# A two-layer graph convolution: unrolled chunks without index copies, dense nodes in pairs of 1024, layer 2 written in node layout

## The reference, cut to what matters

```
x: (100000, 96)   src, dst: (25000,), sorted by dst   edge_attr: (25000, 32)

def conv(x, W_msg, W_edge, W_root, b):
    msg = x[src] @ W_msg + edge_attr @ W_edge
    agg = segment_max(msg, dst, 100000)       # 0 where a node has no edge
    return agg + x @ W_root + b
c1 = leaky_relu(conv(x, W1...));  c2 = leaky_relu(conv(c1, W2...))   # slope 0.01
out = layernorm(x + c2)           # over the 96 features, no scale or bias
```

## Time and profile before

| | us |
|---|---|
| median of 3 runs | 1723.31 |
| fastest, slowest run | 1714.04, 1755.0 |
| profiled execution: span, first to last instruction | 1697.5 |
| around the span, to the median | 25.8 |
| PE busy (in it weight loads, PEld, overlapping) | 978.8 (438.7) |
| DVE busy | 1044.2 |
| ACT busy | 666.9 |
| POOL busy | 1055.8 |
| granted clock of PE, mean | 0.746 |

### The profile page before, as it was taken

How to read it: one execution, slowest core, us unless ns; L and a number is a source line. 1 busy time by engine, 2 the same in 40 slices (tenths; PEclk the granted TensorE clock), 3 DMA queues, 4 the chain that set the end, 5 groups by cost and what they waited for, 6 DMA issues and landing times.

```text
span 1697.5 us, 21367 instructions
## 1 busy us (share of the span) xinstructions
PE 978.8 (58%) x3038; PEld 438.7 (26%) x3038; DVE 1044.2 (62%) x3881; ACT 666.9 (39%) x1717; POOL 1055.8 (62%) x1182
## 2 busy tenths in 40 slices
PE   3476866666666465687778778454343443334441
PEld 1233433233333232332322223222111111111210
DVE  2356666555555465679999999665544555445553
ACT  1345654444444354568888888400000000000000
POOL 5566656455545545617877767666667766677665
PEclk9678877778777777889999999755655655556555
DMA  6366756556555455755444444533333333233320
GB/s 172 93 183 207 240 178 181 174 175 194 175 177 184 146 179 171 220 177 185 157 153 154 152 146 154 164 111 106 104 95 94 107 99 104 79 102 99 107 74 21
DMA packets 142053, 245.87 MB, mean 145 GB/s; under 512 B 31470, under 2 KB 70120, under 8 KB 142022
## 3 DMA queue, kind: packets, MB, share of 16 engines
q1 hardware_dynamic: 103462, 161.26, 30.4%
q0 software_dynamic: 31360, 45.90, 11.5%
q10 hardware_dynamic: 7200, 38.40, 6.0%
HBM read 122.70 MB, written 125.07 MB: 146 GB/s over the span
## 4 chain that ended last, share of the span: by engine, by line
issue 34%; DVE 15%; PE 15%; another core or an unknown queue 15%; ACT 11%; POOL 4%; DMA 1%; DVEq 1%; ACTq 1%; POOLq 1%
ACT ob L686 5%; PE ps L529 5%; PE ps_r L529 4%; DVE stat L820 3%; PE ps_t L519 2%; POOL out L302 2%; PE ps_m L529 2%; DVE c1t L780 2%; DVE mv L831 2%; ACT c2t L647 2%; POOL g_src L295 2%; DVE c2t L780 2%; DVE stage L923 1%; DVE mx L790 1%
## 5 line engine op out<-in xcount | busy, mean ns | idle before, releaser
L686 ACT ACTIVATE ob<-ps_y,shift,rstd 128x96 f32<-128x96 f32 x784 | 273.7, 432 | 139.9 <-DVE shift L859 71.4
L820 DVE BATCH_NORM_STATS2 stat<-ps_y 128x6 f32<-128x96 f32 x784 | 147.0, 248 | 192.4 <-remote 141.1
L302 POOL DMA_INDIRECT agg_table<-stage,now_end x196 | 221.2, 1128 | 68.5 <-issue 68.2
L302 POOL DMA_INDIRECT out<-stage,now_end x196 | 200.4, 1022 | 60.0 <-issue 59.1
L295 POOL DMA_INDIRECT g_src<-in_x,now_gat x196 | 195.8, 999 | 63.0 <-issue 62.9
L295 POOL DMA_INDIRECT g_dst<-in_x,now_gat x196 | 195.2, 996 | 59.7 <-issue 59.1
L529 PE MATMUL ps<-xtb,wr 97*96 97x512 f32 x392 | 224.1, 655 | 11.0 <-ACT c1t L647 2.9
L295 POOL DMA_INDIRECT g_src<-agg_table,now_gat x196 | 196.8, 1004 | 52.9 <-issue 52.6
L529 PE MATMUL ps<-c1t,wr 97*96 97x512 f32 x392 | 212.4, 625 | 11.5 <-issue 10.3
L519 PE MATMUL ps_t<-ident,g_src 128*96 128x128 f32 x392 | 90.2, 374 | 209.9 <-DMA g_src<-agg_table,now_gat 176.7
L655 ACT ACTIVATE std<-mv,epsc 128x4 f32<-128x4 f32 x245 | 74.6, 305 | 296.5 <-issue 185.5
(11 more groups left out here) (54 smaller groups left out, 1494.3 us busy)
## 6 DMA issues: line engine op xcount, KB each, us to landing
xtb<-in_xt SPq DMA_DIRECT2D x196, 192.0 KB
agg_table<-zero ACTq DMA_DIRECT2D x50, 750.0 KB
out<-ob SPq DMA_DIRECT2D x195, 192.0 KB
mask<-mask_row SPq DMA_DIRECT2D x98, 192.0 KB
xd_keep<-g_dst SPq DMA_DIRECT2D x49, 192.0 KB
root_keep<-rt SPq DMA_DIRECT2D x49, 192.0 KB
c1d_keep<-c1d SPq DMA_DIRECT2D x49, 192.0 KB
rt<-root_keep SPq DMA_DIRECT2D x49, 192.0 KB
```

The costliest lines, as they stand in the source:

```text
L302: nc.gpsimd.indirect_dma_start(out=rows, out_offset=bass.IndirectOffsetOnAxis(ap=now_end[:, e.slot(R), r:r + 1], axis=0), in_=stage[:, e.s ...
L686: last = nc.scalar.activation(ob[:, d.slot(R), row(r)], ps_y[k][:, row(r)], ACT.Identity, bias=shift[:, k, r:r + 1], scale=rstd[:, k, r:r ...
L820: last = V.bn_stats(stat[:, k, r, :], rows(r))
```

## The change

- No registers and no loops: every step of every engine is written out, `Step` and `each_chunk` go. POOL's index operand points into src_i, own_i and end_i directly; now_gat, now_end, and POOL's waits for the landing of chunk c-3 go. Scatters read nat directly, stage and yn go.
- Dense work goes by pairs q of PN = 1024 nodes (J = 8 rows per partition, NQ = 98), one pair per tick t; ticks 0 to 48 also have chunk t. xtb and the new xn (x by rows, 3 KB per partition) have four slots, ps_1 and ps_z two banks each and one copy.
- Layer 1: two products, one relu by ACT (`dense_c1`). Leaky(z) is written as 0.99 relu(z) + 0.01 z. Layer 2 uses relu(z1) with 0.99 W2 (w2s) plus [x, 1] with 0.01 W1 W2 and the biases (w12, computed once by two small products), both into one PSUM tile. The operands are swapped: c1t and xtb are the weights, w2s and w12 (96 columns) move, so the result is in node layout and the transposes go.
- The result: ACT writes 0.99 relu(z2) to yo (`dense_c2`), DVE adds 0.01 z2 to xn (`dense_u`), then xn to yo (`dense_y`); DVE normalises four of eight rows, ACT the other four.
- Edges of layer 2: eight short matmuls add c1d with W2_root and the maxima (by the identity) in ps_n; the end is as for the pairs.
- SP keeps own rows at tick t, root and c1d at t-2; the scatters of stage B lag by 4.

```diff
-NB = -(-N // CH)
-LAG = 3
+J = 8
+PN = P * J
+NQ = -(-N // PN)
 R = 4
-XR = 2 * R
+XR = 4
+YR = 4
+LAG = 4
...
+            for c in range(NCH):
+                k = c % R
+                if c >= R:
+                    pool.wait_ge(a_t, c - R + 1)
+                gather(x, src_i, c, g_src, k, l_src)
+                if c >= R:
+                    pool.wait_ge(a_own, c - R + 1)
+                    pool.wait_ge(k_xd[k], 16 * turn(c, R))
+                gather(x, own_i, c, g_dst, k, l_dst)
+
             pool.wait_ge(s_cleared, 16 * NZ)
+            for c in range(NCH):
+                pool.wait_ge(a_nc, c + 1)
+                scatter(table, c, sc_t)
+            pool.wait_ge(sc_t, 64 * NCH)
...
+            for t in range(TICKS):
+                if t + 1 < NCH:
+                    load_edges(t + 1, t + 1, a_r, a_scan)
+                load_pair(t + 2)
+                if t < NCH:
+                    keep_own(t)
+                if 2 <= t < NCH + 2:
+                    keep(t - 2)
+                store_pair(t - 3)
...
+            def layer1(q):
+                pe.wait_ge(l_xt[k], 16 * turn(q, XR) + 16)
+                if q >= 1:
+                    pe.wait_ge(d_c1, q)
+                for h in range(2):
+                    last = nc.tensor.matmul(ps_1[0:D, h, :], wr1[:, :], xtb[:, k, h * CH:(h + 1) * CH],
+                                            start=True, stop=True)
+                last.then_inc(d_1, 1)
...
+            def layer2(q):
+                pe.wait_ge(d_c1, q + 1)
+                if q >= 1:
+                    pe.wait_ge(d_c2, q)
+                    pe.wait_ge(d_u, q)
+                for j in range(J):
+                    nc.tensor.matmul(ps_z[:, j // 4, row(j % 4)], c1t[:, q % 2, cols(j)], w2s[:, :],
+                                     start=True, stop=False)
+                    last = nc.tensor.matmul(ps_z[:, j // 4, row(j % 4)], xtb[:, q % XR, cols(j)], w12[:, :],
+                                            start=False, stop=True)
+                last.then_inc(d_2, 1)
...
@@ PE, tick t @@
+                    forward(g_src[:, k, :], a_t)
+                layer2(t - 1)
+                    forward(g_dst[:, ko, :], a_own)
+                layer1(t)
+                    product(ps_m, wm1[:, :], xe[:, k, :], a_m)
+                    product(ps_r, wr1[0:D, :], xe[0:D, k, :], a_r)
+                    maxima_back(o)
+                    product(ps_r, wr1[0:D, :], xd[:, o % 2, :], a_r1)
...
+            def sums_back(c):
+                for r in range(TPC):
+                    nc.tensor.matmul(ps_n[:, row(r)], c1d[:, k, cols(r)], wr2[:, :], start=True, stop=False)
+                    last = nc.tensor.matmul(ps_n[:, row(r)], mx2[:, c % 2, cols(r)], ident[0:D, 0:D],
+                                            start=False, stop=True)
...
@@ ACT, tick t @@
+                dense_std(t - 2)
+                    copy(xe[0:D, k, :], ps_t[0:D, :], a_xe)
+                    clear(c)
+                dense_c2(t - 1)
+                    copy(xd[:, o % 2, :], ps_t[0:D, :], a_xd)
+                dense_c1(t)
+                dense_norm(t - 2)
+                    copy(rt1[:, k, :], ps_r[0:D, :], a_rc)
+                    copy(nat[:, o * TPC:(o + 1) * TPC, :], ...)
...
@@ DVE, tick t @@
+                dense_u(t - 1)
+                dense_rstd(t - 2)
+                dense_y(t - 1)
+                dense_shift(t - 2)
+                dense_stats(t - 1)
+                dense_norm(t - 2)
+                    scan(c, mx1, k, a_scan)
+                dense_aggr(t - 1)
+                    V.scalar_tensor_tensor(out=c1d[0:D, ko, :], in0=ps_r[0:D, :], ...)
+                    leaky(c1d[0:D, ko, :], c1d[0:D, ko, :], a_c1)
```

More of the change, by code:

```diff
@@ L48 @@
 NZ = N * D // (P * ZCOL)
[L49 to L110, removed]
+assert N * D % (P * ZCOL) == 0 and NZ == NCH + 1 and NQ == 2 * NCH and (N - (NQ - 1) * PN) % J == 0
 def gnn_kernel(nc, x, xt, src, dst, dst_next, dst_row, dst_prev, eat,
@@ L728, in _ @@
-            clear(NZ - 1)
-            each_chunk(act, step_a)
-            maxima(LAST_CHUNK)
-            def step_s(q, s, last=False):
-                c = chunk(q, s)
-                act.wait_ge(a_nc, c.at + 1)
-                if c.reached(2):
-                    act.wait_ge(sc[c.slot(2)], 64 * c.turn(2))
-                copy(stage[:, c.slot(2), :], nat[:, ds(c.at * TPC * D, TPC * D)], s_stage)
-                for t in range(2):
-                    dense(block_s(q, s, t))
-            each_chunk(act, step_s)
@@ L742, in _, with dense_c1 @@
-            for d in DRAIN:
-                dense(d)
-            def sums(c):
-                if c.reached(0):
-                    act.wait_ge(b_n, c.at + 1)
-                    if c.reached(2):
-                        act.wait_ge(ln[EDGE]["done"], c.before(1).at)
-                    copy(yn[:, c.slot(2), :], ps_n[:, 0:TPC * D], b_nc)
-                    norm_std(EDGE, c)
-            each_chunk(act, lambda q, s, last=False: sums(chunk(q, s).before(1)))
-            sums(LAST_CHUNK)
+            def dense_c1(q):
+                if not 0 <= q < NQ:
+                    return
+                act.wait_ge(d_1, q + 1)
+                if q >= 2:
+                    act.wait_ge(d_2, q - 1)
+                nc.scalar.activation(c1t[:, q % 2, :].rearrange("p (h e) -> p h e", h=2), ps_1[0:D, :, :],
+                                     ACT.Relu).then_inc(d_c1, 1)
@@ new lines, in dense_norm @@
+            def dense_norm(q):
+                if not 0 <= q < NQ:
+                    return
+                act.wait_ge(d_shift, q + 1)
+                for j in range(4, J):
+                    last = nc.scalar.activation(yo[:, q % YR, row(j)], yo[:, q % YR, row(j)], ACT.Identity,
+                                                bias=shift[:, q % 2, j:j + 1], scale=rstd[:, q % 2, j:j + 1])
+                last.then_inc(d_done_a, 1)
+            act.wait_ge(w_t, 1)
+            copy(w1t[:, :], ps_t[0:D, 0:D + 1], w_tc)
```

957 lines of the change are left out of this document (422 added, 535 removed).

## The result

The changed kernel takes 2079.13 us (median of 4 runs, 2074.8 to 2081.47) against 1727.42 us for the kernel before (4 runs, 1714.04 to 1755.0): ratio 1.210, 95% interval 1.203 to 1.217. The forecast was 1557 us with a range of 1400 to 1720: wrong, and on the wrong side. The profiled execution has a span of 2079.7 us and a mean granted clock of 0.645.

A forecast was written before the change was run, and what follows sets the result against it. It took POOL's waits for late stores and held-up PE signals to bound the edge stages, DVE the dense stage. 20 start + 627 (A) + 328 (S) + 556 (B) = 1531 us, plus 26: 1557 us, range 1400 to 1720.

The forecast's parts named there:

- The 26 us: Time around the span, added to 1531 us of span; 25.8 us to the median before the change.
- With DVE's 6.25 I take 6.5 us per tick: Dense stage S: PE's chain of 6.4 us and DVE's 6.25 give 6.5 per tick, 328 us in all.
- Rival 2: Layer 2's short products: each load waits for the pass before, 7.8 us per tick, 1920 us in all; chance 0.14.
- It decides from ... 0.18 us per pass: Slow short products in layer 2: from 5.8 us, 0.18 us per pass, the sum reaches 1723 us.
- passes ... some 0.11 us apart at full clock: Sign of a right forecast: spacing of layer 2's short passes on PE, costed at 3.5 us per tick.
- POOL's scatters ... lie beside it: Dense stage S: scatters, at most 6.0 us per step, run beside the 6.5 us tick.
- rival 1: Stages A and B: PE's held-up signals set the rhythm, A stays 745 us, 1719 us in all; chance 0.17.
- the 3.9 us per chunk: Stage A: POOL's wait for the late store of old rows, 189 us in all, loses its cause.
- The ring of slots: Stage A: four slots are late next, adding 2.8 us to 10.0, a tick of 12.8 us.
- 10.0 us, level with POOL: Stage A: PE's time per tick, 8.9 us plus 1.1 for the short products of layer 2.
- The 20 us credited for four chunks gathered ahead: Stage B: POOL ends scatters 30 us before S ends; 16 gathers of 1.25 us off, 576 to 556 us.
- Rival 3: All stages: nothing is late any more, A 505, S 328, B 485, 1364 us in all; chance 0.17.

The follow-up runs named there:

- experiments 5 and 6: 5: changed kernel plus POOL's waits for scatter landings and one unused wide product per dense tick, 1442 us; 6: changed kernel with POOL's index copies back, 1598 us.
- Experiment 1: Changed kernel, but POOL waits for the previous chunk's scatters to land before the next, likewise between stage B's first four gathers: 1816 us.
- experiment 10: Changed kernel plus one unused wide product per dense tick, POOL's break before every second chunk's scatters, one in stage B: 1381.5 us against 1420.9 before, 0.972.
- experiment 3: short_filler: changed kernel plus eight unused products of 96 columns per dense tick behind the last edge chunk, no breaks for POOL: 2174 us.
- experiment 2: Changed kernel with POOL's waits for landings plus two unused products of 512 columns per dense tick: 1617 us, 0.966 of the kernel before.

## Why the prediction was wrong

**Where the 522 us went.** The dense stage took 825 us instead of 328. In the 295 us of held signals PE worked 41, so 254 us are waits; the other 571 are 49 ticks of 11.67 us, 243 more than the 328. That is the excess of 497. Stage B adds 58. Stage A gave 7 back, and what lies around the span was 0 instead of 26. The 26 us were never there: wherever one execution has both numbers, its time is 1.7 to 3.0 us above its span, so nearly all of them were the distance of the profiled execution of the kernel before from its median.

**The step that failed first: "With DVE's 6.25 I take 6.5 us per tick".** It prices PE's chain at full clock, and the stage was granted 0.51. As a chain it was right: at full clock the tick is 6.64 us (experiments 5 and 6). The 3.5 us of layer 2 in it are right too. What was missing is the clock. I took the 0.98 over from the stage before the change, where half of PE's wide products were layer 2's; the change turns just these into short passes. Rival 2 named the short products, "It decides from ... 0.18 us per pass", and the dense stage has 0.2135; but its mechanism (a load waits for the pass before it) did not occur, and it gave 15.9 us for stage A, which took 12.7 at 0.112 per pass. The sign to look for was in the forecast's own list, "passes ... some 0.11 us apart at full clock", with the clock as a condition that was never priced. At 1.2 GHz the same chain is 11.67 us, and 49 x 5.2 us alone give 1810.

**The second: "POOL's scatters ... lie beside it".** The forecast saw that signals come late "while gathers run without a pause" and that the dense stage of the kernel before has none of it, and concluded that scatters are harmless. But POOL was not without breaks there. Its timeline in the kernel before, dense stage:

```profile
804.90 1.01 POOL L302 DMA_INDIRECT agg_table<-stage,now_end  x1 [0.30 <-issue]
806.22 1.43 POOL L302 DMA_INDIRECT agg_table<-stage,now_end  x1 [0.30 <-issue]
807.96 1.02 POOL L302 DMA_INDIRECT agg_table<-stage,now_end  x1 [0.30 <-issue]
808.97 0.21 POOL L316 COPY now_end<-end_i 128x4 int32<-128x4 int32 x1
809.34 1.37 POOL L302 DMA_INDIRECT agg_table<-stage,now_end  x1 [0.17 <-issue]
```

Four scatters take 6.1 us, with a copy among them; after the change four take 5.1, and nothing stands between them. The held-up rhythm was priced for A and B only (rival 1), never for S. Experiment 1 shows that breaks end it, on one chip. Which of the differences had protected the kernel before (copies, pace, or PE's own shorter stream of instructions) was not shown.

**Stage A: right in sum, not in its reason.** POOL's wait for xd_keep is gone, a chunk takes 12.7 us (forecast 12.8), and PE, busy 503 of 620 us, is as loaded as POOL (377 us, and 0.30 between each of its 391 operations). But in free sessions the version with the late store takes the same 10.28 us, so the store's place alone costs nothing. That the 3.9 us per chunk were a consequence of the held signals (late results make SP late, SP's store makes POOL wait) fits this and isn't shown: the late store wasn't tried in a held session, nor the kernel before profiled in a free one. The ring of slots that the forecast put 2.8 us per chunk on is late as it said: POOL waits 103.7 us in 43 times for PE's transposes before its gathers into g_dst, 2.1 us per chunk. In the free session of experiment 10 stage A has no such wait, so the ring is late only where the signals are. The floor came out as forecast: 10.28 us against "10.0 us, level with POOL".

**Stage B: 614 instead of 556.** The row of 277 us in 24 waits is the old one of the earlier trace rows under a new name: every second chunk ACT waits 11.5 us. Where it is absent B takes 10.1 to 10.4 us per chunk, the floor of 10.3. The 20 us credited for four chunks gathered ahead were taken back: from the last dense c2 (1460.17) to the first result of B (1480.71) lie 20.5 us in which the chain of B starts.

**Terms that held.** ACT and DVE of one dense tick, and the table loads of the whole run:

```profile
L505 ACT ACTIVATE c1t<-ps 96x1024 f32<-96x1024 f32 x98 | 99.9, 1019 | 190.0 <-PE ps L394 158.5 <-remote 27.4 <-issue 4.2
...
L514 ACT ACTIVATE yo<-ps_z 128x768 f32<-128x768 f32 x98 | 79.4, 810 | 691.6 <-PE ps_z L408 293.7 <-remote 217.3 <-issue 180.6
...
L497 ACT ACT_TABLE_LOAD x1 | 1.3, 1283 | 9.6 <-PE ps_t L373 9.6
L523 ACT ACT_TABLE_LOAD x1 | 1.3, 1283 | 0.0
```

1.0 and 0.8 us as worked out, DVE 4.86 us per tick (5.1 forecast), two table loads in all: relu costs none. The Trainium skill (ScalarE: Activation LUTs, Table sets) has relu in every set, and the trace agrees. The loads by rows cost nothing: 251 GB/s in stage A, 305 in a free session, and in neither does PE wait for xtb or DVE for xn. The passes of layer 2 come 0.112 us apart at full clock, and 0.2135 at half, 1.9 times that, so their spacing goes with the granted clock. The Trainium skill (TensorE: Matmul & The Clock Gate, LDWEIGHTS) has 107 ns for a load of 128 columns; the 0.112 us at full clock fits it better than the 0.083 of the transposes do.

**Rival 3** ("nothing is late any more", 1364 us: A 505, S 328, B 485) was given 0.17. With the clock up and signals free, experiment 10 has 507, 334 and 520. Its arithmetic was sound for A and S, and 35 us short for B; what it lacked is the clock in the dense stage and, in held sessions, prompt signals.

## What to carry to other kernels

Work out PE's time at the clock that the new mix of work will be granted, and ask for both levels: where half of PE's wide passes give way to passes of 96 columns, a stage can lose its clock although PE is busy all the time (experiment 3), and a wide product that nobody uses can then save time (experiment 2). When a copy or a wait of the engine that issues indirect transfers is removed, ask who lived on its breaks. And a wait seen in one profile can be a consequence of another one: only a run in which the first is gone tells what the second is worth.

## What the runs showed of the hardware

- A stretch of 570 us with PE 100% busy was granted half the clock: 3.4 of each 13.6 us were wide products, the rest passes of 96 columns. 355 us with twice as many wide products per tick were granted all of it, and so were 280 us with one and a half times as many, on the chip of the first stretch. In stage A, where three more wide products and some transposes stand beside the same 32 short passes, the clock was 0.92.
- In held sessions other engines waited for PE up to 94 us (130 in short_filler) while POOL issued indirect transfers without a break, and PE itself stood idle up to 3.9 us between instructions meanwhile. In free ones no profile of the changed code shows it, and the kernel before takes 1417 to 1433 instead of 1657 to 1755 us. Within a session its times agree within 3.3%.
- One break per chunk, for the landing, ended it in the dense stage in the four runs of one session. What in the chip holds the signals back, or slows PE's instructions, stays open.
